# Splits and row turns moved among the last transposes, five early and eleven late shared tiles in place of six and ten

## What is computed

```python
x = x + tanh(g_xattn[0]) * xattn(layernorm(x), ctx, ctx, mask, Wq, bq, Wk, bk, Wv, bv, Wo, bo)
n = layernorm(x)                                  # x2 in the kernel
probs = softmax(n @ gate_w.T); top_w, sel = top_k(probs, 2); top_w /= sum(top_w)
y = sum over the two experts of  top_w * (gelu(n @ W1[e] + b1[e]) @ W2[e] + b2[e])
x = x + tanh(g_ffn[0]) * (y + gelu(n @ sW1 + sb1) @ sW2 + sb2)
```

## Time and profile before

| | |
|---|---|
| median of 3 runs | 572.21 us (568.67 to 574.97) |
| the profiled execution | 573.9 us |
| its span, first to last instruction | 572.3 us |
| granted TensorE clock, mean | 0.964 |
| TensorE busy | 534.5 us (93%) |
| VectorE busy | 370.9 us (65%) |
| POOL busy | 293.9 us (51%) |
| ScalarE busy | 244.6 us (43%) |

### The profile page before, as it was taken

One profiled execution on the slowest core, in us unless ns is written; L12 is line 12 of the kernel. 1 busy time (PEld: TensorE's weight loads), 2 busy tenths in 40 slices (PEclk: granted clock), 3 DMA queues, 4 the chain that ended last, 5 costly groups with the idle time before them and its releaser, 6 DMA issues.

```text
span 572.3 us, 12564 instructions
## 1 busy us (share of the span) xinstructions
PE 534.5 (93%) x3227; PEld 465.3 (81%) x3228; DVE 370.9 (65%) x798; ACT 244.6 (43%) x543; POOL 293.9 (51%) x266
## 2 busy tenths in 40 slices
PE   4989899998977969999999999999999999999996
PEld 3778799997876757888888888888888888888885
DVE  4656866667655598666555566655556565557897
ACT  2434766765553422433433343343434334334342
POOL 8407469896578784333444443443344351045551
PEclk9987999999688699999999999999999999999999
DMA  5442555675452245365755667566767641123342
GB/s 145 123 156 81 167 169 153 186 226 172 141 170 101 103 156 192 129 184 180 221 173 190 184 209 191 174 192 220 198 224 193 216 132 37 37 72 105 108 146 82
DMA packets 56251, 89.27 MB, mean 156 GB/s; under 512 B 6478, under 2 KB 41790, under 8 KB 56230
## 3 DMA queue, kind: packets, MB, share of 16 engines
q0 software_dynamic: 25136, 59.15, 34.9%
q1 hardware_dynamic: 24645, 24.76, 13.5%
q10 hardware_dynamic: 6448, 5.12, 2.8%
HBM read 68.15 MB, written 16.65 MB: 148 GB/s over the span
## 4 chain that ended last, share of the span: by engine, by line
PE 78%; DVE 11%; ACT 5%; issue 4%; DMA 1%; DVEq 0%; ACTq 0%; SPq 0%
PE ps L789 17%; PE ps L776 9%; PE ps L777 9%; PE ps L778 9%; PE ps L790 8%; PE ps L764 8%; PE ps L847 3%; PE ps L803 3%; PE ps L757 2%; PE ps L833 2%; ACT hid L1052 1%; DVE xres L1321 1%; DMA front<-in_ctx 1%; PE ps L858 1%; DVE st L1324 1%
## 5 line engine op out<-in xcount | busy, mean ns | idle before, releaser
L789 PE MATMUL ps<-w2hl,hTh 128*128 (+1 forms) x440 | 160.4, 405 | 3.0 <-DVE hTl L1340 2.8
L1173 ACT ACTIVATE hid<-hid 128x512 f32<-128x512 f32 x110 | 69.0, 632 | 133.6 <-DVE hid L1346 126.9
L790 PE MATMUL ps<-w2hl,hTl 128*128 (+1 forms) x440 | 122.6, 279 | 0.0
L1167 ACT ACTIVATE hTh<-ps 128x512 fp32r<-128x512 f32 x110 | 60.1, 596 | 99.1 <-PE ps L764 95.0
L789 PEld LDWEIGHTS ps<-w2hl,hTh 128*128 128x128 f32 x440 | 82.6, 188 | 21.0 <-issue 3.8
L776 PE MATMUL ps<-w1l,xT 128*128 (+1 forms) x220 | 93.3, 424 | 5.2 <-DVE xT L1334 4.7
L1346 DVE TENSOR_TENSOR hid<-ps,b1bc 128x512 f32<-128x512 f32 x110 | 74.6, 688 | 30.4 <-PE ps L778 22.4
L777 PE MATMUL ps<-w1h,xT 128*128 (+1 forms) x220 | 88.4, 402 | 0.0
L778 PE MATMUL ps<-w1h,xT 128*128 (+1 forms) x220 | 88.1, 400 | 0.0
L790 PEld LDWEIGHTS ps<-w2hl,hTl 128*128 128x128 f32 x440 | 82.9, 189 | 0.0
L1340 DVE TENSOR_TENSOR hTl<-ps,hTh 128x512 fp32r<-128x512 f32 x110 | 70.7, 684 | 5.4 <-ACT hTh L1167 5.4
(11 more groups left out here) (203 smaller groups left out, 853.9 us busy)
## 6 DMA issues: line engine op xcount, KB each, us to landing
stage<-in_L_ffn_W POOLq DMA_DIRECT2D x14, 1024.0 KB, 5.6
w1h<-in_L_ffn_W POOLq DMA_DIRECT2D x7, 1024.0 KB, 5.8
w2hl<-in_L_ffn_W POOLq DMA_DIRECT2D x7, 1024.0 KB
qstack<-moved_q SPq DMA_DIRECT2D x48, 128.0 KB, 2.5
xrow<-routed_x SPq DMA_DIRECT2D x39, 128.0 KB
routed_y<-yrow ACTq DMA_DIRECT2D x39, 128.0 KB, 1.7
moved_q<-hid SPq DMA_DIRECT2D x16, 256.0 KB, 3.3
b1bc<-in_L_ffn_b POOLq DMA_DIRECT2D x8, 512.0 KB, 6.9
```

The lines of the kernel that those rows point to most:

```text
L789: mm(p_y, hTh[:, c, :], part(2 * D), start=c == 0, stop=False)
L790: last = mm(p_y[:, 0:D], hTl[:, c, :], part(D), start=False, stop=c == FC - 1)
L1167: act.activation(hTh[:, n * (FC // 2):(n + 1) * (FC // 2), :], p_hT[:, n, :, :], ACT.Copy).then_inc(S["hT_hi"], 1)
L1173: act.activation(hid[:, n, :], hid[:, n, :], ACT.Gelu).then_inc(S["h_act"], 1)
```

## The change

- `NA` is 5 in place of 6, so there are 11 late tiles; `COMBINED` gets an empty entry ahead of its last three.
- The copies of the value sets are dealt out anew: ScalarE has sets 0, 1, 4, 5, 8, VectorE 2, 3, 6, 7.
- POOL's load of the second half of `x` waits until the queries of tiles 0 and 1 have been moved.
- POOL makes the four splits of the first expert's W1 in step 13, ahead of all scatters, and those of its W2 one by one behind the groups of scatters. One of its loads of W2 goes from step 13 to step 12.
- `p_x` lies in bank 2 for tile 0 and in bank 6 from tile 1 on, in place of bank 5. `turn_rows(0)` waits for the last scores to be read, not for logits.
- TensorE turns the rows of tile 1 in step 16 and runs the two halves of `up(1)` in steps 17 and 18. `rows_hi(1)` and `rows_lo(1)` move with it.
- VectorE does `slots(0)` ahead of the residual in step 13.

```diff
-    NA = 6
+    NA = 5
-        p_x = ps[:, 5, 0:D].rearrange("p (c q) -> p c q", q=P)
+        p_x = lambda i: ps[:, 2 if isinstance(i, int) and i == 0 else 6, 0:D].rearrange("p (c q) -> p c q", q=P)
@@ gpsimd
-            pool.dma_start(xres[:, NT // 2:NT, :], x_v[:, NT // 2:NT, :]).then_inc(S["x_in2"], 16)
             pool.wait_ge(S["gate_tanh"], 1)
...
             key_diag(1, 1)
+            pool.wait_ge(S["q_moved"], 16 * 2)
+            pool.dma_start(xres[:, NT // 2:NT, :], x_v[:, NT // 2:NT, :]).then_inc(S["x_in2"], 16)
             normal(4)
...
                     load_quarter_2(1, first_w2, 0)
+                    load_quarter_2(1, first_w2, 1)
                 if t == 13:
-                    for q in range(1, 4):
-                        load_quarter_2(1, first_w2, q)
+                    load_quarter_2(1, first_w2, 2)
+                    load_quarter_2(1, first_w2, 3)
+                    for q in range(4):
+                        split_quarter_1(1, q)
...
                     scatter(batch, n)
-                if g < 2:
-                    split_quarter_1(1, 2 * g)
-                    split_quarter_1(1, 2 * g + 1)
-                else:
-                    split_quarter_2(1, 2 * (g - 2))
-                    split_quarter_2(1, 2 * (g - 2) + 1)
+                split_quarter_2(1, g)
@@ tensor
-                        pe.wait_ge(S["v_spread" if n % 2 else "v_spread_act"], n // 2 - 1)
+                        pe.wait_ge(S["v_spread" if n % 4 >= 2 else "v_spread_act"], n % 2 + 1 if n < 8 else 3)
...
+            def up_half(i, p, s, n):
+                if n == 0:
+                    pe.wait_ge(S["w1_ready"], p + 1)
+                    pe.wait_ge(S["xT_lo"], i + 1)
+                if not isinstance(i, int) or i >= 1:
+                    pe.wait_ge(S["h_add"], 2 * i - 1 + n)
...
             def up(i, p, s):
                 for n in range(2):
+                    up_half(i, p, s, n)
...
                 if known and t == NT - 1:
-                    pe.wait_ge(S["l_sb"], t - 3)
+                    pe.wait_ge(S["p_sub"], NT)
                     turn_rows(0, 0)
...
-                    if known and t == NT - 1:
-                        pe.wait_ge(S["xT_lo"], 1)
                     turn_x2(t - 3, 1 - parity)
...
                 if known and t == 16:
                     places(1)
+                    pe.wait_ge(S["x1_mid"], NT)
+                    turn_rows(1, 1)
+                if known and t in (17, 18):
+                    up_half(1, 0, 0, t - 17)
...
-            pe.wait_ge(S["l_sb"], NT)
-            turn_rows(1, 1)
-            tile(1, 1, (0, 0), (0, 0), lambda: places(2))
+            turn_hidden(0)
+            places(2)
+            turn_rows(2, 0)
+            down(0, 0, 0)
@@ scalar
+                if isinstance(t, int) and t == 16:
+                    rows_hi(1)
                 if ok(t - 1):
                     deviation(t - 1)
...
-            spread_values(2)
+            spread_values(1)
             exponent(0)
-            for n in range(4, len(SETS), 2):
+            for n in (4, 5, 8):
                 spread_values(n)
...
-                if not known or i < TILES - 1:
+                if not known or 0 < i < TILES - 1:
                     rows_hi(i + 1)
@@ vector
+                if isinstance(t, int) and t == 13:
+                    slots(0)
                 if ok(t + 3):
                     queries_lo(t + 3)
...
                     residual(t - 1)
-                if isinstance(t, int) and t == 13:
-                    slots(0)
...
                 if isinstance(t, int) and t == 16:
                     slots(1)
+                    rows_lo(1)
...
-            for n in range(1, len(SETS), 2):
+            for n in (2, 3, 6, 7):
                 spread_values(n)
...
             choose(2, 1)
-            rows_lo(1)
...
-            COMBINED = ((), (), (0, 1), (2, 3), (4, 5), (6, 7), (8, 9), (10, 11), (12, 13), (14, 15))
+            COMBINED = ((), (), (0, 1), (2, 3), (4, 5), (6, 7), (8, 9), (), (10, 11), (12, 13), (14, 15))
```

More of the change, by code:

```diff
@@ L756, in turn_rows @@
                 for c in range(C):
[L757 removed]
+                    last = nc.tensor.transpose(p_x(i)[:, c, :], xrow[:, parity, c * P:(c + 1) * P], ident[:])
                 last.then_inc(S["xT_ps"], 1)
@@ L765, in turn_hidden @@
                     last.then_inc(S["hT_ps"], 1)
+            def up_half(i, p, s, n):
[4 more added lines that the diff above has]
+                    pe.wait_ge(S["h_add"], 2 * i - 1 + n)
+                part = lambda w, c: w[:, bass.ds(s, 1), c, n * (F // 2):(n + 1) * (F // 2)].rearrange(
+                    "p o f -> p (o f)")
+                for c in range(C):
+                    mm(p_h[:, n, :], xTh[:, c, :], part(w1l, c), start=c == 0, stop=False)
+                    mm(p_h[:, n, :], xTh[:, c, :], part(w1h, c), start=False, stop=False)
+                    last = mm(p_h[:, n, :], xTl[:, c, :], part(w1h, c), start=False, stop=c == C - 1)
+                last.then_inc(S["h_ps"], 1)
             def up(i, p, s):
-                pe.wait_ge(S["w1_ready"], p + 1)
-                pe.wait_ge(S["xT_lo"], i + 1)
                 for n in range(2):
-                    if not isinstance(i, int) or i >= 1:
-                        pe.wait_ge(S["h_add"], 2 * i - 1 + n)
-                    part = lambda w, c: w[:, bass.ds(s, 1), c, n * (F // 2):(n + 1) * (F // 2)].rearrange(
-                        "p o f -> p (o f)")
-                    for c in range(C):
-                        mm(p_h[:, n, :], xTh[:, c, :], part(w1l, c), start=c == 0, stop=False)
-                        mm(p_h[:, n, :], xTh[:, c, :], part(w1h, c), start=False, stop=False)
-                        last = mm(p_h[:, n, :], xTl[:, c, :], part(w1h, c), start=False, stop=c == C - 1)
-                    last.then_inc(S["h_ps"], 1)
+                    up_half(i, p, s, n)
             def down(i, p, s):
```

5 lines of the change are left out of this document (2 added, 3 removed).

## The result

The changed kernel takes 582.96 us (median of 4 executions, 578.39 to 586.64) against 572.30 us of the kernel before, run beside it. The ratio is 1.0187, with a 95% interval of 1.0094 to 1.0279: slower by about 2%. Every ratio in this document leaves out the slow executions of either kernel (those more than 1.5% above the fastest of their kernel), while medians and ranges count all of them, so what one kernel costs against another is taken from the ratios, 0.001 being 0.57 us. The forecast was 565.1 us. The profiled execution took 582.41 us, its span is 580.8 us.

A forecast was written before the change was run, and what follows sets the result against it. TensorE, busy 534.5 of 572.3 us, was taken as the bound, leaving idle time and low clock to win. 573.9 - 4.6 (early clock) - 2.2 (early tiles) - 0.3 (late tiles) = 566.8 us, 565.1 as median; range 560.5 to 572.5.

The forecast's parts named there:

- Rival (e): From 181 us TensorE's clock stays at the lower level through the early tiles; slower, up to 582.8 us; chance 0.05.
- `slots(0)` ... is over just before the first split: Step 13: slots start at 157.2 us, last 1.5 us, just miss POOL's splits; counted at 0, a miss up to 5.0 us.
- The load of the routed rows: Tile 5's 128 KB load, issued at 218.1 us beside 2 MB, takes 4.4 us; early tiles win 2.2 us.
- Rival (b): Routed rows land only with the two large loads, at 224.3 us; total gain 1.1 us, 571.1 us; chance 0.13.
- this chain alone would win 8 us: VectorE's chain after the last choice, through tables and sources to `up(4)` near 217 us, would win 8 us.
- The early clock: At 39 to 49 us: idle cut to 1.8 us no longer drops the clock; with the filled hole, 4.6 us won.
- rival (a): The clock falls at 39 us as before: 1.4 in place of 4.6 us; gain 3.9 us, 568.3 us; chance 0.25.
- Eleven late tiles: Late stage: gathers further ahead and one tile without a combine win 0.3 us, between 0 and 0.6.
- the cast of `phase_of`: In VectorE's tables, with no POOL split beside it: below 0.5 us, 2.5 us less.
- the halves of `up(1)`: Run between the last transposes and ahead of the last logits, pushing the logits to 190.9 us and last choice to 193.5.
- the load of x: Second half of x, waiting for the queries' move, ends some 4 us later but delays nobody: counted 0.
- the wait of 3 to 6 us at the turn of tile 5: Sign: TensorE waits 3 to 6 us for tile 5's rows, released by the DMA.

The follow-up runs named there:

- 4: Kernel before with only five early and eleven late tiles: 577.10 us, ratio 1.013.
- 2: Changed kernel with six early and ten late tiles again: 575.52 us, ratio 1.001.
- 7: Kernel before with only POOL's moved load and splits, and `slots(0)` ahead of the residual: 574.60 us, ratio 1.009.
- 10: Kernel before with only the new order of the value sets, first run: 570.13 us, ratio 0.999.
- 11: Kernel before with only the new order of the value sets, run again: 569.62 us, ratio 0.996.
- 9: Kernel before with only the bank changes, the earlier row turns of tile 1 and the halves of `up(1)`: 571.94 us, ratio 1.002.
- 15: Kernel before with only the load of the second half of x behind the move of the queries: 571.06 us, ratio 0.999.
- 3: Changed kernel with POOL's splits waiting for the first batch's slots, and six early tiles: 568.41 us, ratio 0.998.
- 8: Kernel before with POOL's moves, `slots(0)` ahead of the residual, and the splits waiting for these slots: 569.95 us, ratio 1.000.
- 12: Changed kernel with the value sets in the order of the kernel before: 579.12 us, ratio 1.017.
- guard: One added wait in POOL's queue, keeping the four W1 splits of step 13 behind `slots(0)`; alone on the changed kernel: 578.41 us, ratio 1.011.
- 1: Changed kernel with POOL waiting for the first batch's slots ahead of its four W1 splits: 578.41 us, ratio 1.011.
- 6: Changed kernel, five early tiles, with both the guard and the hold: 575.17 us, ratio 1.010.
- 13: Changed kernel with the guard, six early tiles and the old order of the value sets: 569.34 us, ratio 0.998.
- 14: Changed kernel with the guard and six early tiles, new value order, run again: 568.70 us, ratio 0.999.
- 16: Changed kernel with the guard, six early tiles and the load of x at its old place: 570.77 us, ratio 1.001.
- hold: One added wait keeping POOL's two 1 MB loads back until tile 5's rows are turned; on the kernel before with five early tiles: 575.03 us, ratio 1.006.
- 5: Kernel before with five early tiles, POOL's two 1 MB loads waiting until tile 5's rows are turned: 575.03 us, ratio 1.006.

## Why the prediction was wrong, step by step

**Measured per part**, by the ratios: five for six early tiles +7.2 us (4), or +10.1 us with the rest of the change in (after less 2); POOL's moves with the collision +5.4 us (7); the spread order -0.3 and -2.1 us (10, 11), the halves +0.9 us (9), the load -0.9 us (15), none of these four told from zero. The parts measured alone sum to 10.5 to 12.3 us, and this and the 10.7 us of the whole agree within what these runs can tell.

**The forecast missed by 15.6 us** (582.4 against its 566.8 us for the profiled execution), and the traces split it so. The first 158 us gave 7.4 us: step 13 began 2.8 us later than before (158.40 against 155.57 us on TensorE's timeline), where 4.6 us were to be won. Another 2.2 us were lost by the last logits: they came 5.0 us later than the 190.9 us of the prediction (195.88), 2.8 of which are those of step 13. From there to the turn in tile 4 the prediction had 226.5 - 190.9 = 35.6 us and the trace has 236.19 - 195.88 = 40.3: 4.7 us. The tile behind gave 8.8 in place of 6.7 us: 2.1 us. The late stage was 1.3 us shorter than in the profile before, where 0.3 were forecast: -1.0. Together 15.4 us. This splits one profile of each kernel, and how long the clock stayed low is chance in both, in the first term above all. Rival (e) named 582.8 us, which is nearly the measured time, but that is luck: its mechanism, the lower clock through the early tiles, isn't there. From 186 to 251 us the clock was low for 13.6 us in the kernel after and for 13.4 us in the kernel before.

**"`slots(0)` ... is over just before the first split"** failed. The margin in the working was 0.1 us (slots until 158.7, splits from 158.84); in the trace it was -0.3 us (`slot_f` begins at 161.62, and `slot` would have ended near 162.0; the splits begin at 161.71), after the stretched `onplace` had used up 0.6 us. And the margin goes with the clock. In the four profiles with POOL's moves in which the granted clock was 1.00 at 157 us (after, 2, 3 and 8), the slots begin ahead of the place of the splits. In the other seven it was 0.50 there: POOL came to its splits 1.2 us before the slots began (kernels 7 and 12), or its guard waited 2.8 us (kernels 1, 6, 13, 14, 16). The profile of the kernel before, from which I read the margin, has 1.00 as well. The prediction had named the penalty, up to four splits or 5.0 us, and it came out as 3.83 + 1.18 us; but it priced the step at 0, since "2.4 us of such a slip would be hidden by POOL's own lateness". They were not hidden: the residual stands behind the slots, `normal_two(12)` waits for it, and POOL was idle for 2.92 us. That the last scatter came at 221.32 us and not at 215.4 is these 2.9 us and the 2.8 us of step 13. Kernels 1, 7 and 8 show the price: 4.4 us back with the guard, 5.4 us lost by POOL's moves, 5.3 us back with the guard. And the trace of the kernel before already spoke against any margin of tenths: `xres` began at 201.35 us, 0.5 us ahead of POOL's two splits (201.88, shown above), and would have ended just before them, yet it lasted until 204.70, past the end of the second. The Trainium skill (SBUF — State Buffer, section Who interferes with whom) has the rule that each side shuts out the other for a whole instruction. The trace agrees and goes further: one VectorE instruction (`slot_f`, 3.83 us) waited for three of POOL's in a row.

**The load of the routed rows** was mis-sized: 6.9 us, not 4.4. Rival (b), chance 0.13, had its mechanism, landing with the two large loads: 231.8 us against some 231.6 and 232.4 for these (223.51 and 224.30 plus 8.1). And it was issued late: the prediction took the last scatter (215.4 us) as what releases it, but in the kernel after SP issues it 1.0 us behind `src_row` (223.66), which ran behind an instruction stretched to 1.93 us by POOL's last split. That stretch cost little by itself, since the last scatter had landed only near 223.7 us. In kernel 6 `src_row` was over by 218.1 us, and the last scatter, issued at 219.84, came last. Where the hold takes the company away, the stretch from the last logits to the turn in tile 4 is 229.97 - 194.26 = 35.7 us, which is the prediction's 35.6; so the size came out, in part by luck: the load was issued 29.1 us after the last logits where the prediction had 27.2, it took 2.0 us where it had 4.4, and from the turn of the rows to the end of the tile were 4.6 us where it had 4.0. The Trainium skill (DMA: Bandwidth & Descriptors, section SWDGE vs HWDGE vs iDMA) says that each DMA engine serves its queues in turn. What the prediction drew from it, that the small load should pass with little delay, is not borne out here: 6.9 us beside 2 MB, against 2.0 us without.

**The split behind it** was missing. The prediction ended its chain at tile 4. But the large loads land on time for POOL's `w1l` split of 4.57 us to start at 236.55, just ahead of the residual of tile 4: 2.1 us more. Six tiles put one tile of work there and the split meets something that nobody waits for.

**Six tiles as a cover** was the step behind all this. I took "this chain alone would win 8 us" together with the five tiles and set the sum against the kernel before; I never asked what the same chain gives with six. Kernel 3 has it: the turn of tile 4 at 224.02 us, 4.7 us before that of the kernel before and 2.5 us before my 226.5 us for five. With five tiles or six there are 49 tiles behind tile 5, so the only question is when tile 5 is reached. As a shared tile it needs no routed rows and fills the time in which scatters, sources and load are done; as a routed one it waits for them. And most of the 8 us wasn't the change's to win: in the stretch of the table kernels 10, 11 and 15, which have none of its moves there, are 6 to 7 us shorter than the profile I started from.

**The early clock**, my largest term (4.6 us), is not there. TensorE's wait at L742 was 1.8 us, as worked out, and the clock fell all the same, as in rival (a). The order wins 0.3 and 2.1 us in kernels 10 and 11, around the 1.4 us of that rival but not told from zero. An idle of 1.8 us doesn't decide it: the profile of kernel 10 has two, one that ends at 39.81 us with the fall behind it, and this one, behind which the granted clock stays at 1.00:

```profile
59.54 1.09 PE L815 MATMUL ps<-kd,qstack 97*128 97x154 f32 x8 [1.80 <-issue]
```

How long the clock stays low is not set by the order or the load alone: two profiles of one kernel differ by 13.7 us (10 and 11).

**Eleven late tiles** won nothing: 335.8 us from tile 5 to the end with five and with six. The 1.3 us of the profile before are its own: all other profiles, with five tiles or six, lie within 0.6 us of each other.

**What held:** the cast of `phase_of` took 0.18 us in place of 2.67, though kernels 9, 10, 11 and 15 have that without POOL's moves; the halves of `up(1)` ran ahead of the last logits; the load of x cost 0; the wait of 3 to 6 us at the turn of tile 5 was there (2.9, behind another of 2.27).

**Open:** whether the 4.1 us residual of tile 4 would cost its 2.1 us with every other loss cured; it was not tried apart from the hold. What stretched `onplace` and the share of the large loads in the cost of the five tiles are open too. No kernel here beats the kernel before beyond doubt: the lowest ratio is 0.996 (kernel 11), and 1 lies inside its interval.

## What to carry to other kernels

Work that looks movable can be the cover of a transfer: before taking a tile from ahead of a dependent load, add up what it hides (last write, address, load, whatever runs on the queue beside it) and price the load with the company it will have. A margin of tenths of a microsecond in an argument of order is no margin; either put a wait in place (the guard gave 4.4 and 5.3 us where the splits could collide, and cost nothing measurable) or price the miss in full. And a term that rests on the clock not falling after a shorter idle should be forecast as zero with a range, since it varies between executions of one kernel by more than the term. The same holds for a collision read from a single profile: before counting its removal as a gain, take a second profile of the unchanged kernel and see whether the collision is there.

## What the runs showed of the hardware

- A VectorE instruction on 128x16 elements that starts 0.09 us ahead of a row of four POOL splits of 1.23 us each took 3.83 us, until the end of the third; the next, with one input, took 1.18 us, until the end of the fourth. Undisturbed they take 0.17 us each.
- A load of 128 KB from SP's queue took 2.0 us (kernel 6) and 2.1 us (kernel 5) with no large load beside it, and 4.5 us (kernel 1), some 5.7 us (kernel 4) and 6.9 us (after) beside two loads of 1 MB from POOL's queue. The large ones took 6.7 to 8.1 us there.
- The stretch at the lower TensorE clock that begins near 40 us lasted from 6.8 to over 20 us (6.8 and 20.5 us in two profiles of one kernel, 10 and 11). In the profile with 6.8 us a second idle of 1.8 us was followed by no fall. Executions of the kernel before lie between 565.2 and 580.7 us in sets of 28 to 35, and with a dozen executions of a kernel beside them the interval of a ratio was still some 0.005 to each side.
